# A Mamba block and two transformer layers over 16 elements: first and last elements specialised, order made anew

## What is computed

```python
# Mamba block on the normalised x: D_INNER 256, 16 states, conv of 4 taps, dt of rank 8
xb, z = split(layernorm(x) @ in_proj_w, 2)
xb = silu(causal_depthwise_conv(xb, conv_w, conv_b))
proj = xb @ x_proj_w                                   # 8 + 16 + 16 columns
dt = softplus(proj[..., :8] @ dt_proj_w + dt_proj_b);  b, c = proj[..., 8:24], proj[..., 24:]
state = exp(dt * -exp(A_log)) * state + dt * b * xb    # along the 512 tokens
y = (sum_over_states(state * c) + D_param * xb) * silu(z)
x = x + layernorm(y @ out_proj_w)
# two layers of local attention (8 heads of 64, windows of 64, keys of this and the last window)
h = layernorm(x)
for l in range(2):
    q, k, v = split(shift_token(h) @ wqkv[l], 3)       # q, k: norm over a head, scale, rotary
    h = h + softmax(mask(q @ k.T)) @ v @ wo[l]
    a, g = split((layernorm(shift_token(h)) * lg + lb) @ w1[l] + b1[l], 2)
    h = h + (a * gelu(g)) @ w2[l] + b2[l]
x = x + layernorm(h)
```

## Time and profile before

| | |
|---|---|
| median of 3 runs | 2424.35 us (2414.93 to 2427.51) |
| profiled execution | 2425.17 us, span 2423.4 us, 43963 instructions |
| busy: PE, DVE, ACT, POOL | 1934.9, 1914.2, 1741.6, 1716.1 us (80%, 79%, 72%, 71%) |
| scans | 512 x 1217 ns on VectorE, 623.3 us |
| dbu and gy on GpSimd | 512 x 1274 and 512 x 1275 ns, 1304.9 us |

### The profile page before, as it was taken

How to read it: one execution, slowest core, us unless ns; L and a number is a source line. 1 busy time by engine, 2 the same in 40 slices (tenths; PEclk the granted TensorE clock), 3 DMA queues, 4 the chain that set the end, 5 groups by cost and what they waited for, 6 DMA issues and landing times.

```text
span 2423.4 us, 43963 instructions
## 1 busy us (share of the span) xinstructions
PE 1934.9 (80%) x15823; PEld 1138.6 (47%) x15936; DVE 1914.2 (79%) x3509; ACT 1741.6 (72%) x3891; POOL 1716.1 (71%) x1572
## 2 busy tenths in 40 slices
PE   2255889798988979797988979797988979788866
PEld 0012446363635446363645546363644536364634
DVE  3557797979889797988888797988889797987442
ACT  2245778696978778696877879696877869686644
POOL 1959596877959596886959596895959597792110
PEclk9967999998999999899999989999999999899988
DMA  5444343535345453535434353534434353541000
GB/s 167 126 114 119 107 119 96 131 101 145 100 118 131 107 123 89 142 82 151 113 110 122 108 125 95 142 91 132 124 105 119 106 133 94 140 104 34 17 16 14
DMA packets 126346, 261.09 MB, mean 108 GB/s; under 512 B 26928, under 2 KB 59696, under 8 KB 125872
## 3 DMA queue, kind: packets, MB, share of 16 engines
q1 hardware_dynamic: 126128, 258.27, 40.4%
HBM read 185.42 MB, written 42.99 MB: 94 GB/s over the span
## 4 chain that ended last, share of the span: by engine, by line
PE 37%; ACT 18%; DVE 18%; POOL 14%; issue 10%; DMA 2%; SPq 0%; POOLq 0%; DVEq 0%; ACTq 0%
POOL dbu L663 5%; POOL gy L680 5%; ACT late L893 4%; DVE m L928 4%; PE b_bank L357 3%; PE f_bank L357 3%; ACT da L609 3%; DVE kr L942 3%; PE b_bank L763 2%; POOL kr L997 2%; PE y_sum L584 2%; PE b_bank L780 2%; PE b_bank L746 2%; PE f_bank L746 2%; PE f_bank L763 2%
## 5 line engine op out<-in xcount | busy, mean ns | idle before, releaser
L629 DVE TENSOR_TENSOR_SCAN hs<-da,dbu 128x512 f32<-128x512 f32 x512 | 623.3, 1217 | 112.5 <-POOL dbu L663 67.6
L680 POOL TENSOR_TENSOR gy<-hs,bc 128x512 f32<-128x512 f32 x512 | 652.7, 1275 | 34.2 <-DVE hs L629 21.8
L663 POOL TENSOR_TENSOR dbu<-spread,bc 128x512 f32<-128x512 f32 x512 | 652.2, 1274 | 16.5 <-DMA spread<-steps 16.5
L609 ACT ACTIVATE da<-spread,rest 128x512 f32<-128x512 f32 x512 | 362.3, 708 | 140.2 <-DVE hs L629 121.1
L720 PE MATMUL b_bank<-rest,h_t 128*128 128x512 f32 x384 | 245.8, 743 | 75.4 <-DVE kr L942 71.5
L997 POOL TENSOR_TENSOR kr<-kr,rn 128x512 f32<-128x512 f32 x256 | 261.0, 1044 | 32.9 <-ACT rn L853 18.4
L720 PE MATMUL f_bank<-rest,h_t 128*128 128x512 f32 x384 | 235.8, 717 | 40.2 <-DVE kr L942 30.4
L584 PE MATMUL y_sum<-gy,rest 128*32 128x512 f32 x1024 | 146.4, 647 | 93.3 <-POOL gy L680 93.3
L357 PE MATMUL b_bank<-first,kr 128*128 128x128 f32 x768 | 127.5, 291 | 82.3 <-DVE kr L942 60.4
L893 ACT ACTIVATE late<-b_bank,mx 128x128 f32<-128x128 f32 x512 | 141.0, 383 | 60.5 <-DVE mx L958 60.5
L1146 POOL TENSOR_TENSOR xs<-xs,v 128x512 f32<-128x512 f32 x16 | 18.9, 1183 | 215.9 <-ACT xs L352 215.9
(11 more groups left out here) (171 smaller groups left out, 4789.3 us busy)
## 6 DMA issues: line engine op xcount, KB each, us to landing
spread<-steps SPq DMA_DIRECT2D x256, 512.0 KB, 4.7
vs<-v SPq DMA_DIRECT2D x96, 260.0 KB, 5.6
steps<-k_t SPq DMA_DIRECT2D x32, 512.0 KB, 3.0
bc<-bc_rows SPq DMA_DIRECT2D x32, 512.0 KB, 6.4
gate<-gates SPq DMA_DIRECT2D x32, 512.0 KB, 5.4
gates<-kr SPq DMA_DIRECT2D x16, 512.0 KB, 2.9
gates<-late SPq DMA_DIRECT2D x16, 512.0 KB, 3.9
vs<-v SPq DMA_DIRECT2D x32, 130.0 KB, 4.7
```

Of the source, the lines that this page charges most:

```text
L609: e.activation(da[:, :], spread[:, slot(b, s // 2), 0, :], ACT.Exp, scale=a_neg[:, s:s + 1]).then_inc(decayed.sem, 1)
L629: e.tensor_tensor_scan(hs[:, s % 2, :], da[:, :], dbu[:, s % 2, :], 0.0, ALU.mult, ALU.add).then_inc(scanned.sem, 1)
L663: e.tensor_tensor(dbu[:, s % 2, :], spread[:, slot(b, s // 2), 1, :], bc[:, s % 2, :], ALU.mult).then_inc(fed.sem, 1)
L680: e.tensor_tensor(gy[:, s % 8, :], hs[:, s % 2, :], bc[:, 2 + s % 2, :], ALU.mult).then_inc(read_out.sem, 1)
```

## The change

**Order.** `ORDER` has three words per engine now: the first covers what five rounds did, the second is repeated eleven times, the third covers the rest. All three are woven anew; the counts per round in the middle are the same as before.

**Entry of element 0** (`entry_bank`). Its products go to five banks: i0, i1, i2 to f_bank0 to 2, i3 to b_bank0, the 40-row product to b_bank1, the dt products to f_bank0 and 1. The four in products wait for `xn_t` alone, the 40-row product for the SILUs of u alone. The four products of `pool_steps` are made by VectorE (`step_inputs`, called in `dve_enter`), ahead of `dve_tables`.

**Scans of elements 0 and 1.** `by_dve(b, s)` gives read-out products to VectorE: in element 0 those with s % 3 > 0 (21 of 32), in element 1 those with s % 3 == 1 (11 of 32); one stands behind the scan after its own. da alternates between bank `da` and b_bank0 (`decay`), so ScalarE waits for the scan two back.

**Layer 1 of the last element** (`bank_list`). It goes round eight banks: the three of its own, `da`, `y_sum` and the three of A; take n waits for take n-8. Squares go to `gy`, rotated q tiles to `bc`, so that waits for `summed` and `turned` go. Heads have two pairs of score banks and two value banks: `score(1)` stands in front of the first transposes, `score(g+2)` behind the values of pair g; out projection in bank `da`.

```diff
+        def entry_bank(b, part):
+            if b:
+                return e_bank
+            return dict(turn=e_bank, i0=fa[0], i1=fa[1], i2=fa[2], i3=lb[0], x=lb[1], d0=fa[0], d1=fa[1])[part]
...
             for i, before in enumerate((e_copied(b), conv_step(b, 2), conv_step(b, 5), z_made(b, 0))):
-                E.wait_ge(*before)
+                E.wait_ge(*(before if b else e_copied(0)))
...
-            E.wait_ge(*z_made(b, 1))
+            E.wait_ge(*(z_made(b, 1) if b else u_made(0, 1)))
...
+                if b == 0 and h == NH2 - 1:
+                    for _ in step_inputs(E, e, 0):
+                        pass
...
+        def by_dve(b, s):
+            return b < SHARED and (s % 3 > 0, s % 3 == 1,)[b]
+        def decay(b, s):
+            return lb[0] if b < 2 and s % 2 else da
...
-                if s:
+                if s and decay(b, s) is decay(b, s - 1):
                     E.wait_ge(*scanned(b, s - 1))
+                elif s > 1:
+                    E.wait_ge(*scanned(b, s - 2))
...
+                if s and by_dve(b, s - 1):
+                    read_product(E, e, b, s - 1)
+                if s == NSCAN - 1 and by_dve(b, s):
+                    read_product(E, e, b, s)
...
+                if not by_dve(b, s):
+                    read_product(E, e, b, s)
...
+            def bank_list(self, b):
+                if self is wb and b == B - 1:
+                    return [*lb, da, y_sum, *fa]
+                return self.banks
+            def head_banks(self, b):
+                L = self.bank_list(b)
+                if len(L) == 3:
+                    return [L[0:2]] * 4, [L[2]] * 8
+                return [L[0:2], L[3:5]] * 2, [L[2], L[5]] * 4
...
-                    E.wait_ge(*w.p_copied(b, 2 * g - 2))
-                    E.wait_ge(*w.p_copied(b, 2 * g - 1))
+                    E.wait_ge(*w.p_copied(b, 2 * g - (3 if wide else 1)))
...
-                if hd:
-                    E.wait_ge(*w.o_done(b, hd - 1))
+                if hd > wide:
+                    E.wait_ge(*w.o_done(b, hd - 1 - wide))
```

220 lines of the change are left out of this document (144 added, 76 removed), and 80 rows, old and new, of the table ORDER.

## The result

The changed kernel takes 2483.34 us in the median (2480.96 to 2488.05), the kernel before 2419.64 beside it: the ratio is 1.0261, with a 95% interval of 1.0230 to 1.0292. It is 2.6% slower; forecast were 2370 us, 2% faster. The profiled run has a span of 2479.1 us, 55.7 more than before.

The account below looks back on a forecast made before the run. GpSimd's scan phase plus a gap of chains makes each 137 us period; start and end are latency and one-sided load. Terms 12.4 + 10.8 + 5 + 4 + 6.5 + 15.5 = 54.2 off 2424.35: 2370 us, range 2343 to 2395.

Parts of the forecast that it names:

- Part 1: Entry of element 0: separate banks and VectorE's sums and products gain 12.4 us, between 9 and 13.
- Part 2: Scans of element 0 with the read-out shared: 2.07 us per scan, gaining 10.8 us, between 5 and 22.
- Rival (a): Scans of elements 0 and 1: engines don't exclude each other, gains 22 and 8 us, total 2355; chance 0.12.
- (c): Element 0's scans: loads bind them, so sharing the read-out gives nothing, total 2381 us; chance 0.08.
- Part 3: Between elements 0 and 1: earlier convolution, VectorE's last read-out and earlier clips gain 5 us, 2 to 7.
- T + 17.6: Between elements 0 and 1: GpSimd's four products reach 17.6 us after element 0's last scan ends (T), against 22.9 before.
- Part 4: Scans of element 1: a third of the read-outs leaves GpSimd, gaining 4 us, -2 to 7.
- Part 5: The 13 periods: dbu ahead of kr less small losses nets 0.5 us each, 6.5 us in all, -10 to 15.
- A stall here counts thirteen times: The periods: a warning that any stall in the new weave is paid in each of 13 periods.
- Part 6: Last layer on eight banks: rotation 8 us, heads 7, projection out 0.5, together 15.5 us, 8 to 19.
- (b): Last layer and periods: TensorE at 1.2 GHz, new weave costing 0.5 us a period, total 2388; chance 0.15.
- (d): Each period's first dbu: SyncE's dt store blocks later stores; slower from 5.7 us delay, 2448 at 7.5; chance 0.04.

Follow-up runs that it names:

- old_rows_dbu_first: old_rows_2_to_15 with one GpSimd exchange, an element's first dbu product ahead of B's kr step 1: 2381.02 us, ratio 0.9837.
- both_exchanges: Changed kernel with SyncE's residual load back behind the value loads and TensorE's A step 56 ahead of dt projection E 7: 2422.20 us, ratio 1.0008.
- old_rows_2_to_15: Changed kernel with the order of the kernel before from the end of element 1's states to the end of element 15's: 2379.24 us, ratio 0.9825.
- five_rows_new: old_rows_2_to_15 with the changed kernel's repeated rows on all five engines: 2468.43 us, ratio 1.0193.

## Why the prediction was wrong, point by point

**Part 1, entry: 12.4, right, if 1 us low.** GpSimd's four sums and products, now on VectorE, end at 32.6 (forecast 34.7); the first scan starts at 43.6 (45 to 46) and the first gy ends at 47.1, against 60.7: 13.6 us gained, just above the bound of 13.

```profile
31.29 1.29 DVE L524 TENSOR_TENSOR k_t<-k_t,late 128x512 f32<-128x512 f32 x2
45.82 1.27 POOL L633 TENSOR_TENSOR gy<-hs,bc 128x512 f32<-128x512 f32 x1 [1.06 <-DMA bc<-bc_rows]
```

**Part 2, states of element 0: 10.8, right.** First to last gy takes 65.9 us; 65.7 were forecast, from 2.07 per scan with the two engines excluding each other. They do, and it is GpSimd that pays: VectorE's 21 products take 0.68 in the mean, but GpSimd's dbu products 1.40, its gy products have a median of 1625 ns in these states (a mean of 1275 over the whole run before), and a dbu product that meets one of VectorE's takes 1.57. Rival (a), no exclusion, is out, and so is (c): behind the first, no dbu product of element 0 waits for a load. (The exclusion takes half of this part's gain, 22 down to 10.8, not the third that the prediction says.) What the prediction drew from the Trainium skill on products with two SBUF inputs (SBUF — State Buffer, Who interferes with whom) agrees with these rows.

```profile
L633 POOL TENSOR_TENSOR gy<-hs,bc x11: 1261/1625/1628, 45.8 to 110.6; 128x512 f32<-128x512 f32 x11
...
61.74 0.67 DVE L633 TENSOR_TENSOR gy<-hs,bc 128x512 f32<-128x512 f32 x1
...
61.97 1.57 POOL L801 TENSOR_TENSOR dbu<-spread,bc 128x512 f32<-128x512 f32 x1 [0.24 <-DVE hs L763]
```

**Part 3, between elements 0 and 1: 5, wrong by 8.6 us.** The stretch grew by 3.6. I counted GpSimd's dt products down to T + 17.6; they begin at T + 15.9 (128.22) and end at T + 20.8, and I left out what stands between them and dbu. VectorE's four pieces of xs run beside them already here, 4.00 us instead of 1.11 before; what that costs wasn't tried by itself. The rows for dbu landed at 141.2, but GpSimd has B and A steps in front:

```profile
143.36 0.25 POOL L1161 TENSOR_SCALAR ss<-ss 128x16 f32<-128x16 f32 x1 [10.22 <-DVE ss L1085]
144.28 2.04 POOL L1170 TENSOR_TENSOR kr<-kr,rn 128x512 f32<-128x512 f32 x2 [0.67 <-ACT rn L1011]
146.28 2.50 POOL L801 TENSOR_TENSOR dbu<-spread,bc 128x512 f32<-128x512 f32 x2
```

**Part 4, states of element 1: 4, right, if low.** They gained 11.3 and the stretch behind them lost 4.7, 6.6 net; the undone sharing puts 7.0 us of the 11.3 on it. Mechanism right, size within the range.

**Parts 1 to 4 together:** 32.2 forecast, 27.1 measured at element 2.

**Part 5, the periods: 6.5 forecast, 97 lost. This is the step that failed**, in three ways. The gain in it, dbu ahead of kr, was read from GpSimd's idle hole alone; `old_rows_dbu_first` shows that the period does not depend on the first dbu in that order. In the changed kernel the first scan starts 3.0 to 3.1 us behind the start of the first dbu in the elements 4 to 13, against 1.4 to 2.0 before, and VectorE is not idle in between: steps of A and B stand in front of it. Here is the scan of element 9, whose first dbu starts at 1274.64:

```profile
1277.77 1.22 DVE L763 TENSOR_TENSOR_SCAN hs<-da,dbu 128x512 f32<-128x512 f32 x1
```

(The term is also added up wrong: 1.2 gained less 0.9 is 0.3 a period, not 0.5, so 4 us and not 6.5.) The losses that I looked for, SyncE's stores, did not hold the first dbu: its rows land 3.0 to 4.3 us ahead of it in the changed kernel. Their order was never undone by itself, and in `both_exchanges`, where the stretch is shorter, the first dbu does wait 0.2 to 2.0 us for that load. What SyncE did cost was the load of the residual, later in the same row, which I never priced: 19 us. And VectorE's pieces beside GpSimd's products, the largest single term (about 40 us), were open in the earlier trace rows: I had found there that a small VectorE instruction waits for GpSimd's product, and asked this only of the instructions that the change adds, not of those that it shifts. The Trainium skill has the rule for them too (SBUF — State Buffer, Who interferes with whom): `tensor_scalar` can enter a mode with both ports and then contends with GpSimd for its whole length. The trace agrees: 0.34 us alone, 1.3 beside a product; the mode itself is in no row. "A stall here counts thirteen times" was right, and the range of -10 to 15 us was the error: it allowed a stall of 0.8 us a period, and nothing in the profile had bounded what a new weave of some 2500 instructions a period on five engines can do.

**Part 6, last layer: 15.5, right.** 16 us by the medians with the banks undone, 12.6 by the profiled ends; 4.8 for rotation where 8 were forecast, 6.7 for heads and projection where 7.5 were.

**Rivals.** (b) had the right kind of thing, waits of the weave and TensorE's clock together, and put it at 0.5 us a period; it was 7.5. (d) foresaw the direction, and SyncE in order behind a wait, but named the wrong transfer, and SyncE's load is only some 20 of the 97 us. It asked for 5.7 us a period from one stall; the loss is a sum of smaller ones on several engines.

**The budget.** Changed kernel 2483; the xs pieces 41, SyncE's load 20 more (2422, `both_exchanges`). Another 43 lie between that and `old_rows_2_to_15` (2379). By the two profiled runs 17 of them are in the last two elements (the third row; `five_rows_new` says 15), 9 in elements 2 and 3, 21 in elements 4 to 13. Of these 21, six more elements of the long kind would make 13, if the clock is the cause; the rest stays open. The ends gained 41 against 2420; without part 5 the forecast would have been 2424 - 48 = 2376.
